# One visit for both key tiles of the values, cross queries split by ScalarE and GpSimd, output biases by GpSimd, and experts picked from the logits

## The reference

```python
x = x + _L0_attn_ref(_layernorm(x), Wq, Wk, Wv, Wo)          # 16 heads of 8, causal, rotary
x = x + _L0_xattn_ref(_layernorm(x), ctx, W_kv, W_q, W_proj, b_proj)   # 16 heads of 8, no mask
x = x + _L0_ffn_ref(_layernorm(x), gate_w, w1, b1, w2, b2)
...
seq_rep = hidden_states.mean(axis=1)                         # one routing decision for a sequence
probs = softmax(seq_rep @ gate_w)                            # 8 experts
top_w, top_i = top_k(probs, 2)
top_w = top_w / top_w.sum()
...
hmid = gelu(h @ w1[e] + b1[e])                               # 128 -> 512
y = hmid @ w2[e] + b2[e]                                     # 512 -> 128
out = out + combine[:, e] * y
```

## Time and profile before

| | before |
|---|---|
| median of 3 runs | 216.89 us |
| lowest, highest | 216.25, 220.49 us |
| the profiled execution | 217.31 us |
| its span, first to last instruction | 215.4 us |
| mean granted TensorE clock | 0.937 of full speed |
| TensorE matmul busy | 184.6 us |
| VectorE busy | 144.2 us |
| ScalarE busy | 102.9 us |
| GpSimd busy | 51.7 us |

### The profile page before, as it was taken

One profiled execution on the slowest core, in us unless ns is written; L12 is line 12 of the kernel. 1 busy time (PEld: TensorE's weight loads), 2 busy tenths in 40 slices (PEclk: granted clock), 3 DMA queues, 4 the chain that ended last, 5 costly groups with the idle time before them and its releaser, 6 DMA issues.

```text
span 215.4 us, 4233 instructions
## 1 busy us (share of the span) xinstructions
PE 184.6 (86%) x1568; PEld 117.7 (55%) x1568; DVE 144.2 (67%) x345; ACT 102.9 (48%) x218; POOL 51.7 (24%) x93
## 2 busy tenths in 40 slices
PE   0792097969899899998998998999999998999984
PEld 0462063456466565744654644645555554998974
DVE  3599948885465678599889888789866464353200
ACT  2252010005465465554645765767665665873341
POOL 4647805518000020030030030011131341243020
PEclk9999555587999999999999999999999999999999
DMA  5715657126325511611621521400330250340700
GB/s 146 220 37 143 163 155 209 30 76 138 81 79 134 146 55 41 169 55 38 157 68 38 151 72 41 110 3 6 92 104 8 51 146 3 91 130 2 220 24 24
DMA packets 18259, 19.68 MB, mean 91 GB/s; under 512 B 1976, under 2 KB 15808, under 8 KB 17088
## 3 DMA queue, kind: packets, MB, share of 16 engines
q1 hardware_dynamic: 18240, 19.43, 33.3%
HBM read 15.56 MB, written 3.67 MB: 89 GB/s over the span
## 4 chain that ended last, share of the span: by engine, by line
PE 54%; DVE 21%; DMA 15%; SPq 4%; issue 3%; POOL 1%; ACT 1%; POOLq 0%; DVEq 0%; ACTq 0%
PE psA L754 10%; PE psV L802 9%; DMA stackQ<-scratch 8%; PE psB L781 7%; PE psV L869 6%; DVE negmax L537 5%; PE psM L812 3%; PE psA L847 3%; DMA stackQ<-maxT 3%; PE psM L690 3%; PE psA L759 2%; DMA scratch<-hid 2%; PE psV L863 2%; PE psM L822 2%; SPq L315 2%
## 5 line engine op out<-in xcount | busy, mean ns | idle before, releaser
L644 ACT ACTIVATE E<-psB 128x512 f32<-128x512 f32 x112 | 62.6, 597 | 52.7 <-PE psB L786 30.2
L537 DVE TENSOR_REDUCE negmax<-psA 128x2 f32<-128x512 f32 (+1 forms) x112 | 73.0, 683 | 15.5 <-PE psA L759 13.2
L754 PE MATMUL psA<-stackK,stackQ 72*128 72x256 bf16 (+1 forms) x256 | 47.1, 280 | 9.2 <-DVE negmax L537 6.4
L781 PE MATMUL psB<-stackQ,stackK 74*128 74x256 bf16 (+1 forms) x256 | 41.6, 262 | 1.4 <-DMA stackQ<-maxT 1.3
L754 PEld LDWEIGHTS psA<-stackK,stackQ 72*128 72x128 bf16 x256 | 21.0, 104 | 29.4 <-DVE negmax L537 19.6
L802 PE MATMUL psV<-E,V 128*9 128x256 f32 (+1 forms) x512 | 36.2, 355 | 0.0
L781 PEld LDWEIGHTS psB<-stackQ,stackK 74*128 74x128 bf16 x256 | 23.7, 99 | 7.6 <-DMA stackQ<-maxT 2.0
L413 POOL TENSOR_SCALAR rstd<-mv 128x2 f32<-128x2 f32 x12 | 2.8, 231 | 104.1 <-DVE mv L495 104.0
L690 PE MATMUL psM<-ident,xn 128*128 128x128 f32 x24 | 5.8, 338 | 15.0 <-DVE xn L500 14.9
L759 PE MATMUL psA<-mask,ident 128*128 128x256 bf16 (+1 forms) x48 | 18.0, 375 | 0.0
L869 PE MATMUL psV<-w2s,hid 128*128 128x128 f32 x128 | 16.8, 280 | 0.0
(11 more groups left out here) (106 smaller groups left out, 236.6 us busy)
## 6 DMA issues: line engine op xcount, KB each, us to landing
stackK<-scratch SPq DMA_DIRECT2D x24, 192.0 KB
stackQ<-scratch SPq DMA_DIRECT2D x8, 576.0 KB
scratch<-hid SPq DMA_DIRECT2D x12, 192.0 KB, 2.0
w1s<-w_dram SPq DMA_DIRECT2D x8, 258.0 KB, 2.7
w2s<-w_dram SPq DMA_DIRECT2D x8, 256.0 KB, 2.9
scratch<-parts_ctx SPq DMA_DIRECT2D x4, 192.0 KB, 7.8
res<-x_dram SPq DMA_DIRECT2D x4, 128.0 KB, 3.2
ctx_tok<-ctx_dram SPq DMA_DIRECT2D x1, 512.0 KB, 5.3
```

Of the source, the lines that this page charges most:

```text
L537: dve.tensor_reduce(negmax[:, b, h:h + nh, t], psA[:, bank].rearrange("p (h k) -> p h k", h=nh), AX_X, ALU.max, negate=True).then_inc(a_ta ...
L644: act.activation(dst, psB[:, bank].rearrange("p (h q) -> p h q", h=dst.shape[1]), ACT.Exp, scale=SCALE).then_inc(b_taken, 1)
L754: last = pe.matmul(psA[:, bank, i * keys:(i + 1) * keys], stackQ[0:ROWS, b, h, t * P:(t + 1) * P], stackK[0:ROWS, b, h, 0:keys], start=(s ...
L781: last = pe.matmul(psB[:, bank, i * n:(i + 1) * n], stackK[:, b, h, t * P:(t + 1) * P], stackQ[:, b, h, q0:S], start=(s == 1 or i == 0), s ...
```

## The change

It has four parts.

1. `values` is one step for a group: where the second key tile was visited, both are done one after the other.
2. In `q_cross` ScalarE copies the product to `qc`, and GpSimd does the split. VectorE has no part in it.
3. The bias rows of the two experts are read into all 128 partitions. GpSimd scales them, adds them, and adds the sum to `res`; the products with the row of ones are gone. As there is one buffer for them, SyncE waits for the sum of one sequence before it reads the next one's.
4. VectorE takes the two largest logits and their places right from the logits, and GpSimd raises e to one difference. SyncE reads both places before it issues any load, and issues both `w1`, then both `w2`, then both bias rows.

```diff
-        if 0 <= n < NJOB * NG:
-            order.append(("values", *divmod(n // NG, NB), n % NG, h))
+        if h == 1 and 0 <= n < NJOB * NG:
+            order.append(("values", *divmod(n // NG, NB), n % NG))
...
                 if kind == "route_pick":
                     sp.wait_ge(chosen, b + 1)
-                    for k in range(TOPK):
+                    chosen_e = [sp.value_load(top_i[0:1, b, k:k + 1], min_val=0, max_val=NE - 1) for k in range(TOPK)]
+                    for k, e in enumerate(chosen_e):
                         n = b * TOPK + k
-                        e = sp.value_load(top_i[0:1, b, k:k + 1], min_val=0, max_val=NE - 1)
...
+                    if b > 0:
+                        sp.wait_ge(bias2_added, b)
+                    for k, e in enumerate(chosen_e):
+                        b2_expert = w2[bass.ds(e, 1), FF:FF + 1].rearrange("e o d -> (e o) d")
+                        sp.dma_start(b2all[:, k, :], b2_expert.partition_broadcast(P)).then_inc(b2_in[b], 16)
...
                 if kind == "q_cross":                       # GpSimd
+                    bank, k = misc[0]
+                    pool.wait_ge(misc_taken[bank], k)
+                    split(qc[:, b % 2], parts[:, b, 0], parts_q[b])
                     if b == 0:
                         pool.wait_ge(bproj_in, 16)
...
-                    pool.tensor_tensor(small[:, b, 1], euler[:, :], small[:, b, 0], ALU.pow).then_inc(probs_ready, 1)
+                    pool.tensor_tensor(small[:, b, 1, 0:1], euler[:, 0:1], small[:, b, 0, 0:1],
+                                       ALU.pow).then_inc(probs_ready, 1)
...
                     for k in range(TOPK):
-                        pool.tensor_scalar(b2row[:, b, k], b2row[:, b, k], small[0:1, b, 6, k:k + 1], None,
-                                           ALU.mult).then_inc(b2_scaled, 1)
+                        then(pool.tensor_scalar(b2all[:, k], b2all[:, k], small[:, b, 6, k:k + 1], None, ALU.mult))
+                    then(pool.tensor_tensor(b2all[:, 0], b2all[:, 0], b2all[:, 1], ALU.add))
+                    both = b2all[:, 0:1, :].to_broadcast([P, NT, D])
+                    pool.tensor_tensor(res[:, b], res[:, b], both, ALU.add).then_inc(bias2_added, 1)
...
-                if kind == "q_cross":                       # VectorE
-                    ...
-                    then(dve.tensor_copy(dst[:, 0], psM[:, bank, 0:S]))
-                    dve.tensor_tensor(qq, psM[:, bank, 0:S], dst[:, 0], ALU.subtract).then_inc(misc_taken[bank], 1)
-                    dve.wait_ge(misc_taken[bank], k)
-                    then(dve.tensor_copy(dst[:, 1], qq))
-                    dve.tensor_tensor(dst[:, 2], qq, dst[:, 1], ALU.subtract).then_inc(parts_q[b], 1)
...
+                    then(dve.max(v[:, 4], psM[:, bank, 0:NE]))                      # route
+                    dve.max_index(top_i[:, b, :], v[:, 4], psM[:, bank, 0:NE]).then_inc(chosen, 1)
+                    dve.tensor_tensor(v[:, 0, 0:1], v[:, 4, 1:2], v[:, 4, 0:1], ALU.subtract).then_inc(misc_taken[bank], 1)
...
                 if kind == "moe_out":
                     dve.wait_ge(down_done, 2 * TOPK * (b + 1))
+                    dve.wait_ge(bias2_added, b + 1)
...
+                if kind == "q_cross":                       # ScalarE
+                    bank, k = misc[0]
+                    act.wait_ge(misc_full[bank], k)
+                    if b >= 2:
+                        act.wait_ge(parts_q[b - 2], NPART)
+                    act.activation(qc[:, b % 2], psM[:, bank, 0:S], ACT.Copy).then_inc(misc_taken[bank], 1)
...
-                        pe.wait_ge(b2_scaled, TOPK * (b + 1))
-                        for t in range(NT):
-                            for k in range(TOPK):
-                                pe.matmul(y[:, t * P:(t + 1) * P], ones[0:1, :], b2row[:, b, k, :],
-                                          start=(t == 0 and k == 0), stop=False, skip_group_check=True)
```

More of the change, by code:

```diff
@@ L417, in _ @@
             for st in steps:
-                kind, s, b, g, misc = st["kind"], st["s"], st["b"], st["g"], st["misc"]
+                kind, s, b, g, misc, unit = st["kind"], st["s"], st["b"], st["g"], st["misc"], st["unit"]
+                job = s * NB + b
                 if kind == "ln_stats":
@@ L577, in _ @@
                     dve.wait_ge(probs_ready, b + 1)
[L578 to L583 removed]
+                    then(dve.tensor_scalar(v[:, 5, 0:1], v[:, 1, 0:1], 1.0, None, ALU.add))
+                    then(dve.reciprocal(v[:, 6, 0:1], v[:, 5, 0:1]))
+                    dve.tensor_tensor(v[:, 6, 1:2], v[:, 6, 0:1], v[:, 1, 0:1], ALU.mult).then_inc(weights_ready, 1)
                     dve.wait_ge(weights_ready, b + 1)
@@ L645, in _ @@
                                    scale=SCALE).then_inc(b_taken, 1)
-                if kind == "values" and st["u"] == 1:
+                if kind == "values":
                     grp = job * NG + g
@@ L789, in _ @@
                 if kind == "values":
[L790 to L806 removed]
+                    grp = job * NG + g
+                    if grp >= 2:
+                        pe.wait_ge(v_taken, grp - 1)
+                    if g == 0:
+                        taken("v_self" if s == 0 else "v_cross", s, b)
+                    if grp == 0:
+                        pe.wait_ge(v_init, 1)
+                        pe.wait_ge(v_zeroed, 1)
+                    pe.wait_ge(b_taken, b_units_until(grp))
+                    for t in range(NT):
+                        q0 = P if s == 0 and t == 1 else 0
+                        for i in range(GH):
+                            last = pe.matmul(psV[i * VW:i * VW + VC, grp % 2, q0:S], V[:, s, b, t, g * GH + i, :],
+                                             E[:, grp % 3, i, t, q0:S], start=(t == 0), stop=(t == 1),
+                                             skip_group_check=True, tile_position=(0, i * VW))
+                    last.then_inc(v_full, 1)
                 if kind == "o_turn":
@@ L869, in _ @@
                             last = pe.matmul(y[:, t * P:(t + 1) * P], hid[:, n % NHID, c, t * P:(t + 1) * P],
-                                             w2s[:, n % NW, c, :], start=False,
+                                             w2s[:, n % NW, c, :], start=(s == 0 and c == 0 and t == 0),
                                              stop=(s == TOPK - 1 and c == NC - 1), skip_group_check=True)
```

41 lines of the change are left out of this document (7 added, 34 removed).

## The result

The changed kernel took 221.44 us (median; 218.62 to 221.78) against 216.57 for the kernel before (216.02 to 220.49, four runs of each); ratio 1.021, 95% interval 1.012 to 1.030. The forecast was 208.0, range 204.8 to 212.0. The medians are of all runs, the ratios leave disturbed runs out, and where too few others were left, none is given.

A forecast was written before the change was run, and what follows sets the result against it. TensorE nearly bounds the kernel, VectorE now and then holding it back. Terms 0.4 - 1.5 - 3.1 + 0.3 - 0.85 - 4.35 = -9.1 us took the profiled 217.31 to 208.2, a median of 208.0; range 204.8 to 212.0.

The forecast's parts named there:

- Rival 2: Late queries idle TensorE 2 us at each of four boundaries and the clock may fall: 219.8 us, chance 0.05.
- The read of the stack: Cross queries' read from scratch into stackQ: 4.5 us from issue to end of traffic, leaving 2.2 us to spare before.
- The keys behind the read: Next job's key reads, behind the queries on SyncE's queue: a whole job of slack, so no cost was counted.
- The clock: TensorE's clock may drop to 1.2 GHz behind waits from 2 us on, losing 1.7 us of work each time.
- The wait taken as covered: New wait of about 0.8 us for cross queries, hidden until 0.85 us by waiting for VectorE's next result.
- The visits: TensorE's value steps: with both key tiles in one visit, the next product follows about 0.98 us after its start.
- The wait of 0.94: TensorE's wait in a cycle while VectorE splits the queries: 0.94 us, to go with the split off VectorE.
- The first part: Up to 74.83 us: a later maxima transpose delays the stack read, +0.4 us (bounds 0 and 0.43).
- second stretch: 74.83 to 107.50 us: -1.9 from some 7 visits' overheads, +0.4 for the first late queries, -1.5 us together.
- Late queries: Cross queries reaching TensorE late at four boundaries: +0.3 us in all, bounds 0 and 2.5.
- The merge: Both key tiles in one value visit: saves 0.21 us each, 0.46 a cycle after 0.38 lost waiting for VectorE.
- The experts: Expert stage without bias products, with earlier choice of experts: -4.35 us together.

The follow-up runs named there:

- e5: after with eight unused products (1.7 us in all) ahead of a cross job's wait for its queries; 211.45 us, ratio 0.979.
- e6: after with a cross job's stack read early from the self job's parts, so cross queries do not enter the scores; 207.06 us, ratio 0.957.
- after: The changed kernel, all four parts applied to the kernel before; 221.44 us, ratio 1.021.
- e9: after with the next job's keys read later, behind the write of the row maxima; 216.38 us, ratio 0.995.
- e7: after without the merge: one value visit for each key tile, as before; 219.6 us, ratio 1.019.
- e1: after with the query split back on VectorE; 212.8 us, no ratio given.
- e2: The kernel before with only both key tiles of the values in one visit; 217.6 us, ratio 0.992.
- e4: The kernel before with the experts' edits alone; 212.2 us, ratio 0.971.
- e10: e1 with seven unused products in TensorE's wait behind the query split; 212.0 us, ratio 0.978.
- e12: e4 with four unused products in TensorE's wait behind the query split; 213.2 us, ratio 0.984.
- e8: after with the next job's keys issued right ahead of the queries' read; 230.13 us, ratio 1.057.
- e11: after with the split shared by VectorE and GpSimd, keys read later and six unused products; 212.2 us, ratio 0.983.

## Why the prediction was wrong

Rival 2, late queries and the clock, is what happened: 219.8 by its working, 221.4 measured. It had a chance of 0.05. Its two terms hold as well: 4.8 us uncovered, 4.8 measured from e5 to e6, and 6.8 us of clock, 6.7 lost in the two windows of the profile (9 by e5). That the clock's term comes out so near is in part luck: it priced four equal falls, the profile has three of unequal length.

- **The read of the stack** is the step that failed: "its traffic ends about 139.45 [...]: 4.5 us from issue". The end of traffic is not the time at which the waiting product is let go. From issue to release it is 5.57 us in after with nothing behind it, 5.21 to 5.84 in e9. So before there were not 2.2 us to spare but 6.67 - 5.5 = 1.2, and at the last boundary the forecast wait of 0.8 comes out at 1.8, and 1.88 was measured. I gave that read a bound of "0.3 slower". A row that lets a product go was there, the wait of the earlier trace rows. Its read was issued at 66.28, between two groups of key reads (the row is below), and let TensorE go at 74.83. That is 8.55 us, a warning that 4.5 was too little and that keys on the same queue matter. With these 1.1 us more the forecast's own sum gives the measured wait of the last boundary, so the split, the place of the product and the earlier need were sized right there.

```profile
66.28 0.77 SPq L307 DMA_DIRECT2D stackQ<-scratch  x1
```

- **The keys behind the read** "have a whole job of slack": true of the keys, but they share the queue, and cost the queries' read 0.1 to 1.2 us at three of four boundaries (e9), and more when they go first (e8). Together with the read itself, and at the first boundary a write of 2.64 us, that makes the waits 2.25, 3.20 and 2.45.
- **The clock** was weighed only as part of a rival, "from a 2 us wait on"; the forecast's wait was 0.8. With waits of 2.25 to 3.20 it fell, and that cost some 8 to 9 us (e5), nearly twice what the waits themselves do (4.8). The rival priced both at 11.6 for four waits; together they were 14. In e7 one wait of 1.99 cost 10 us. What the rival named, TensorE: Matmul & The Clock Gate, section What's actually happening, in the Trainium skill, agrees with these traces: a stretch with TensorE busy for 2.19 of 4 us was followed by one at half speed, and unused products in the same place kept the clock at 1.00. The 20 us at 0.50 in e7, with TensorE busy throughout, do not agree with it so simply.
- **The wait taken as covered** "until 0.85 us" was sized about right: the 8.8 us of late queries in e5 less four times 0.85 are 5.4, and from e5 to e6 4.8 were measured. In e6, without late queries, TensorE waits 0.60 for VectorE in every cycle, and in e5 0.18 at most at that place. But that is thin cover for an error of 1.1 us at one boundary and up to 2.4 at another, and what lay above it cost the clock besides.
- **The visits** were right: 138.55 to 139.53 is 0.98. The wait of 0.94 is gone. In e6, four pairs in a row wait for VectorE by 0.43 together (0.38 forecast), and its cycles are 15.33, 15.02, 15.69 and 15.16 us, where I had 15.8.
- **The first part**: the projection at 73.02 stands where it did (73.06), but the wait behind it ended at 75.72, 0.9 later than in the earlier trace rows where I had 0.4. The maxima's transpose is at 60.68, 1.02 later and not 0.43, and the read is issued 1.10 later (67.38).
- **The sum** has slips that decide nothing. The -1.9 of the second stretch is more than its own product, 8 x 0.21 = 1.68. Late queries are "+0.3 in all" in the text and 0.4 and 0.3 in the stretches. And the bounds that are named do not reach down to 206 (208.0 - 0.7 - 0.4 = 206.9).
- **The merge** gains what I worked out only where nothing else is late. With the queries on GpSimd it makes the waits longer (0.62, 0.72 and 1.99 in e7; 2.25, 3.20, 2.45 and 1.88 in after). That e7 (1.019) and after (1.021) take the same time is chance as far as these runs show: e7 waits less, but its one fall of the clock lasts longer. With the queries on VectorE the merge uncovers the split (0.94 to 1.48).
- **The experts** were right. From the last projection to the end of the span before took 215.4 - 188.22 = 27.2 us, after 216.8 - 193.66 = 23.1: -4.0 against -4.35. The last `w1` at 201.50 is 196.06 when the 5.44 by which the last projection is later are taken off (196 forecast). Here the forecast's list of signs was careless: its "near 196" and "near 200" leave out the 4.75 us that its own sum gained before the experts.
- **The split on GpSimd** took 2.36 us, as in the earlier trace rows, and began 0.14 behind the copy. The exclusive lock that the Trainium skill names (SBUF — State Buffer, section SBUF: two separate sides) was not put to the test: beside the split VectorE ran only reductions that read PSUM (L541, 2.49 us for four from 140.49, as before).

Open is what the clock costs behind waits of 0.9 to 1.5 us. It fell behind some of them in the profiles of e1, e2 and e4, none of which is the fastest execution of its kernel, and filling them (e10, e12) gave nothing that these runs can tell from none. Open too is a version with the gain of all parts: those that compute the whole layer and beat the kernel before end between 0.971 (e4, the experts' part alone) and 0.984, and their intervals overlap.

## What to carry to other kernels

Measure a transfer from its issue to the start of the instruction that it releases, on a boundary where that instruction does wait, and not to the end of its traffic; then look at what is issued right behind it on the same queue. If the new wait on TensorE could come near 2 us with the error of that sum, price the clock with it: here the clock cost nearly twice what the waits did, and in e7 a single wait of 1.99 us cost 10. A part of a change that shortens TensorE's work makes every round trip through memory more urgent by as much, so its gain has to be set against the slack of the longest one.

## What the runs showed of the hardware

- A read of 576 KB from scratch takes 5.2 to 5.8 us from issue to release with no other read right before or behind it on its queue (after, e9), 5.7 to 6.8 with another 576 KB issued right behind it (after, e7), and 7.7 to 8.1 with them right ahead (e8). A write of 192 KB takes 2.0 us alone, and 2.8 to 3.9 in e11, where 576 KB of reads were issued 3 to 6 us ahead of it.
- Order on a queue did not shield the first: what was issued right behind slowed it too, by 0.1 to 1.2 us at three boundaries (after against e9).
- Unused products, 1.7 us of them in each of four waits, made a kernel 9 us faster (after 1.021, e5 0.979).
- The length of a wait does not decide alone whether the clock falls. It fell behind waits of 2.25 to 3.20 us (after), 1.99 (e7), 1.48 (e1, after a window in which TensorE was busy for 0.94 of 2 us) and even 0.60 (e10), and stayed at 1.00 behind 1.88 (after, 150.72), 0.94 (before) and each 0.60 of e6.
- Nor is the price fixed: the granted clock was under 1.00 for some 3 to 7 us behind the waits of after, and at 0.50 for 20 us behind the one of 1.99 in e7, with TensorE busy all the time.
